# Padded staging rows for the weights, and an earlier order for tile 1's rows, means and two flags

## What is computed

```python
x = x + attention(layernorm(x), ctx, ctx, mask)     # causal mask and key mask, softmax over 256 keys
def ffn(x):                                          # x: (8, 256, 256), after a layernorm
    h = silu(tlin(x, w1, s1)) * tlin(x, w2, s2)      # 256 -> 1024
    h = gelu(tlin(h, h1, hs1))                       # 1024 -> 1024
    h = gelu(tlin(h, h2, hs2))                       # 1024 -> 1024
    return tlin(h, w3, s3)                           # 1024 -> 256
x = x + ffn(layernorm(x))                            # tlin(x, w, s) = (x @ w.T) * s
```

## Time and profile before

| | us |
|---|---|
| median of three timed executions | 370.94 (370.41 to 371.08) |
| the profiled execution's own time | 372.69 |
| its span, first to last instruction | 370.7 |
| TensorE matmul busy | 361.4 (98%) |
| TensorE weight load busy | 304.6 (82%) |
| VectorE busy | 177.9 (48%) |
| ScalarE busy | 147.0 (40%) |
| GpSimd busy | 33.9 (9%) |
| mean granted TensorE clock | 0.997 |

### The profile page before, as it was taken

How to read it: one execution, slowest core, us unless ns; L and a number is a source line. 1 busy time by engine, 2 the same in 40 slices (tenths; PEclk the granted TensorE clock), 3 DMA queues, 4 the chain that set the end, 5 groups by cost and what they waited for, 6 DMA issues and landing times.

```text
span 370.7 us, 4744 instructions
## 1 busy us (share of the span) xinstructions
PE 361.4 (98%) x1786; PEld 304.6 (82%) x1786; DVE 177.9 (48%) x405; ACT 147.0 (40%) x247; POOL 33.9 (9%) x59
## 2 busy tenths in 40 slices
PE   8899999999999999999999999999999999999994
PEld 7787887878798888888898888888889888888884
DVE  4857425245456652443655752434545652323323
ACT  4799743843135622251143642161122653121210
POOL 7450130000100031000000004000010000000000
PEclk9999999999999999999999999999999999999998
DMA  7899999992710001000331000000001000000001
GB/s 246 324 387 430 355 355 391 387 371 69 242 58 16 3 0 28 2 0 0 110 147 58 1 0 30 0 0 2 0 0 57 2 3 0 0 0 2 0 2 60
DMA packets 12739, 38.34 MB, mean 103 GB/s; under 512 B 2114, under 2 KB 5060, under 8 KB 12356
## 3 DMA queue, kind: packets, MB, share of 16 engines
q1 hardware_dynamic: 11840, 37.12, 27.2%
q10 hardware_dynamic: 868, 0.80, 0.8%
HBM read 35.80 MB, written 13.64 MB: 133 GB/s over the span
## 4 chain that ended last, share of the span: by engine, by line
PE 93%; DVE 3%; ACT 1%; issue 1%; POOL 0%; DVEq 0%; POOLq 0%
PE ring L975 60%; PE ring L949 15%; PE ring L994 8%; PE att L902 2%; PE att L921 2%; PE ring L1107 1%; PE att L892 1%; DVE turned L600 1%; PE att L910 1%; ACT work L476 0%; DVE x_attn L714 0%; DVE h_lo L657 0%; ACT act L517 0%; PE att L1134 0%; DVE h_hi L765 0%
## 5 line engine op out<-in xcount | busy, mean ns | idle before, releaser
L975 PE MATMUL ring<-h_hi,weights 128*128 128x512 f32 x512 | 201.5, 394 | 1.1 <-DVE seg_flags L739 0.9
L975 PE MATMUL ring<-h_lo,weights 128*128 128x512 f32 x512 | 199.4, 390 | 0.0
L975 PEld LDWEIGHTS ring<-h_hi,weights 128*128 128x128 f32 x512 | 96.1, 188 | 21.7 <-issue 1.6
L975 PEld LDWEIGHTS ring<-h_lo,weights 128*128 128x128 f32 x512 | 96.2, 188 | 19.7
L517 ACT ACTIVATE act<-ring,scales 128x512 f32<-128x512 f32 x64 | 44.1, 690 | 160.7 <-PE ring L975 157.2
L765 DVE CAST h_hi<-act 128x512 fp32r<-128x512 f32 x64 | 27.6, 430 | 145.8 <-ACT act L517 137.8
L657 DVE TENSOR_TENSOR h_lo<-act,h_hi 128x512 fp32r<-128x512 f32 x96 | 66.2, 689 | 2.6
L949 PE MATMUL ring<-xn_hi,weights 128*128 128x512 f32 (+1 forms) x140 | 51.6, 375 | 0.2 <-DVE xn_lo L733 0.2
L949 PE MATMUL ring<-xn_lo,weights 128*128 128x512 f32 (+1 forms) x140 | 51.1, 371 | 0.0
L505 ACT ACTIVATE gate<-ring,scales 128x512 f32<-128x512 f32 x32 | 22.0, 689 | 33.7 <-PE ring L949 33.6
L754 DVE SCALAR_TENSOR_TENSOR act<-ring,scales,gate 128x512 f32<-128x512 f32 x32 | 24.0, 749 | 17.4 <-PE ring L949 16.0
(11 more groups left out here) (128 smaller groups left out, 217.5 us busy)
## 6 DMA issues: line engine op xcount, KB each, us to landing
weights_staged<-in_weights SPq DMA_DIRECT2D x22, 512.0 KB, 8.7
weights<-weights_staged SPq DMA_DIRECT2D x22, 512.0 KB, 7.6
x_in<-in_x SPq DMA_DIRECT2D x8, 256.0 KB, 2.9
ctx_cols<-in_ctx_cols SPq DMA_DIRECT2D x8, 256.0 KB, 4.8
ctx_rows<-in_ctx_rows SPq DMA_DIRECT2D x4, 512.0 KB, 7.6
out_dram<-residual SPq DMA_DIRECT2D x16, 128.0 KB, 1.7
turned<-in_x_cols SPq DMA_DIRECT2D x3, 512.0 KB, 8.3
mask<-in_mask SPq DMA_DIRECT2D x3, 256.0 KB
```

What stands on the lines that cost most here:

```text
L975: ins = nc.tensor.matmul(bank[:], w, part[:, k].bitcast(dt), start=(k == 0 and part is h_hi[src]), stop=(k == HC - 1 and part is h_lo[src]))
```

## The change

The staging tensor gets rows of 1040 elements of which 1024 are used. Tile 1's rows are issued right behind raw piece 5, ahead of the load of piece 6. VectorE makes their statistics in the last four gate and up chunks of tile 0 (one row each), and their mean and variance after (0, 0). The means are stored at (0, 0) and spread at (0, 2); the queries are centred after (0, 5). The tests of pieces 14 to 21 each move one chunk forward (14 from (0, 6) to (0, 5), 15 and 16 from (0, 7) to (0, 6), 17 from (1, 0) to (0, 7), and so on). Flag HID2B is taken ahead of (1, 0) instead of (1, 1), and LAST ahead of (1, 6) instead of (1, 7). All of it concerns tile 0 alone, but for the row length.

```diff
-    staged_d = nc.dram_tensor("weights_staged", [PIECES, P, PIECE], F32).ap()
+    staged_d = nc.dram_tensor("weights_staged", [PIECES, P, PIECE + 16], F32).ap()[:, :, 0:PIECE]
 # SyncE
             load_raw(4)
             load_raw(5)
+            sp.wait_ge(x_attn_done, ROWS)
+            load_queries(1)
...
-                if n == FLAG_PIECES[HID1A][1]:
-                    sp.wait_ge(x_attn_done, ROWS)
-                    load_queries(1)
 # ScalarE
-                        if more and (layer, c) == (0, 2):
+                        if more and (layer, c) == (0, 0 if t == 0 else 2):
                             store_means(t + 1)
-                        if more and (layer, c) == (0, 3):
+                        if more and (layer, c) == (0, 2 if t == 0 else 3):
                             spread_means(t + 1)
...
-            after = ((0, 0), (0, 0), (0, 1), (0, 1), (0, 2), (0, 3), (0, 4), (0, 6), (0, 7), (0, 7), (1, 0), (1, 1),
-                     (1, 2), (1, 3), (1, 4))
+            after = ((0, 0), (0, 0), (0, 1), (0, 1), (0, 2), (0, 3), (0, 4), (0, 5), (0, 6), (0, 6), (0, 7), (1, 0),
+                     (1, 1), (1, 2), (1, 3))
 # VectorE
+            def next_stats(t, r):
+                if r % 2 == 0:
+                    dve.wait_ge(x_loaded[r // 2], 16 * (t + 1))
+                norm_stats(r, x_in)
...
+                    if t == 0 and c >= HC - ROWS and c < HC:
+                        next_stats(1, c - HC + ROWS)
...
-                        for flag, before in ((HID1B, (0, 2)), (HID1C, (0, 4)), (HID2A, (0, 7)), (HID2B, (1, 1)),
-                                             (HID2C, (1, 4)), (LAST, (1, 7))):
+                        for flag, before in ((HID1B, (0, 2)), (HID1C, (0, 4)), (HID2A, (0, 7)), (HID2B, (1, 0)),
+                                             (HID2C, (1, 4)), (LAST, (1, 6))):
...
-                        if at == (0, 1):
+                        if at == (0, 0 if t == 0 else 1):
                             wait_stats(t + 1, 0, ROWS - 1)
...
-                        if at == (0, 0):
+                        if t > 0 and at == (0, 0):
                             for r in range(ROWS):
-                                if r % 2 == 0:
-                                    dve.wait_ge(x_loaded[r // 2], 16 * (t + 2))
-                                norm_stats(r, x_in)
-                        if at in ((0, 1), (1, HID2_CHUNKS[2][0])):
+                                next_stats(t + 1, r)
+                        if at in ((0, 0 if t == 0 else 1), (1, HID2_CHUNKS[2][0])):
                             for r in range(ROWS):
                                 norm_moments(r)
-                        if at == (0, 6):
+                        if at == (0, 5 if t == 0 else 6):
                             for b in range(PAIR):
                                 centre(t + 1, b)
```

## The result

| | before | after |
|---|---|---|
| median of thirteen timed executions, us | 371.08 (369.82 to 372.92) | 368.97 (368.08 to 370.19) |
| profiled execution: own time, span, us | 372.69, 370.7 | 368.78, 366.6 |

The ratio after to before is 0.9937, with a 95% interval of 0.9917 to 0.9956: 2.3 us less, 1.6 to 3.1.

A forecast was written before the change was run, and what follows sets the result against it. TensorE was taken as the bound throughout (matmuls fill 361.4 of 370.7 us). Lost time -1.76, statistics +0.15 and raw piece 3 +0.06 sum to -1.55: from 370.94 to 369.4 us, range 368.8 to 370.7.

The forecast's parts named there:

- The lost time: TensorE's waits for late flags in tile 0 go: scores(1) 0.38, HID2B 1.03, LAST 0.35 us, together -1.76 us.
- The statistics: Four 0.35 us operations on VectorE in gate and up delay TensorE's matmul at 37.45: +0.15 us (0 to 0.6).
- Raw piece 3: Its load stands behind piece 7's slower staging and ScalarE waits for it: +0.06 us (0 to 0.7).
- The padding: Staging in 128 packets of 4 KB instead of 16 of 32 KB takes 0.12 us longer a piece (0 to 1.47).
- The means and tile 1's rows: Means stored and spread earlier, tile 1's rows issued 1.90 us ahead of piece 6's load with 4.0 us cover: cost 0.
- The cover of the tests: ScalarE's test of piece 17 may begin as late as 66.8, piece 17 landed at 60.8: 6.0 us of cover, cost 0.
- Rival C: Slow staging delays ScalarE's test of piece 17; kernel slower from 0.54 us more a piece, up to 384 us; chance 0.09.

The follow-up runs named there:

- e3: Kernel before with only the tests of pieces 14 to 21 and flags HID2B and LAST a chunk earlier: ratio 0.9950, compared trace stretch 1.75 us shorter.
- e4: Kernel before with only tile 1's rows, statistics, means and centring earlier: ratio 0.9986, compared trace stretch 0.47 us shorter.
- e7: Changed kernel with each of the four statistics in gate and up made twice: compared trace stretch 84.96 us, against 84.43 for the changed kernel.
- e5: Changed kernel with staging rows cut into runs of 256 elements, so packets of 1 KB: ratio to the kernel before 0.9943.
- e8: Changed kernel with chunks (0, 0) to (0, 2) in one branch instead of two: ratio to the kernel before 0.9944, compared trace stretch 2.39 us shorter.

## Why the prediction came out as it did

The mechanism was right: three late flags, two because VectorE took them behind work that waited for ScalarE, one because the centring stood in front; e3 and e4 part them as forecast, and nothing took the waits' place at these three. The size was low, 1.55 for 2.0, and the step that failed is the sum: each of its three terms was mis-sized, the first of them most.

- **The lost time, 1.76: measured 2.01.** I counted the distance between the last matmul and the next less 0.23. The distances did close as forecast (0.39, 1.03, 0.35). But the successor of a matmul behind a stop comes later too. In the kernel before, behind HID2B, the weight load and the two matmuls:

```profile
76.09 0.19 PEld L975 LDWEIGHTS ring<-h_hi,weights 128*128 128x128 f32 x1 [1.29 <-issue]
76.10 0.49 PE L975 MATMUL ring<-h_hi,weights 128*128 128x512 f32 x1 [0.88 <-DVE seg_flags L739]
76.43 0.40 PE L975 MATMUL ring<-h_lo,weights 128*128 128x512 f32 x1
```

  That is 0.33 behind 76.10, where 0.23 is usual. The weight load, else one distance ahead of its matmul, starts with it here. Matmul by matmul against the changed kernel, the successors give 0.11, 0.10 and 0.05 us beside the distances: 0.49, 1.15 and 0.38 at the three places, together 2.01. The page's idle times (0.22, 0.88, 0.20) are too low still, since the modelled ends cover part of the gap.
- **The statistics, +0.15: measured 0, at the place named by its slack and in the sum by luck.** What TensorE asks for, and when, was right: e7's weight load waits for the last low part. The end of that low part was wrong: 0.85 us later than before was forecast, and counted from the start of the stretch it is 0.43 later (12.34 for 11.91), because chunk 5's product began 0.36 earlier (6.84 for 7.20). That the edit didn't do; raw piece 4 was late in the execution profiled before and not in the one after (see e3). And the price has a place that the prediction didn't look at: the second statistic holds the flag HID1A back, 0.20 us on TensorE against e3. The late raw piece 4 had held the same flag as long in the kernel before, so the two cancel in the difference. Against an execution of the kernel before with raw piece 4 in time the change would gain some 1.75 us; that is an estimate from e3, of which there is one trace.
- **Raw piece 3, +0.06: measured 0.** The row of ScalarE's wait (1.14 us) was right, and it does sit at the edge of TensorE's path. But what moves it is the landing of that load, 0.2 to 2.1 us of wait from one execution to the next, padded or not.
- **The padding, 0.12 us a piece:** the four kernels without it average 100.9 us of engine time, the eight with rows of 1040 or 1088 and packets of 4 KB 102.1. That is 0.06 a piece, half the forecast, and the two groups overlap (100.3 to 101.7, 100.4 to 103.6). As it was covered, the sum didn't suffer.
- **The means and tile 1's rows:** right. The load of piece 6 is issued 1.1 us later (19.02), of its cover of 4.0; the centring is done at 61.2 as forecast. The cover of the tests was smaller than worked out, 3.1 us at piece 17 for 6.0, since piece 17 landed 1.5 us later than before and was tested at 65.37 and not at 66.8. Rival C's point was wrong by the other factor: not every microsecond of engine time reaches the landing (3.2 of 8.0 in e5).
- **The range:** its lower end allowed 0.35 us beyond 1.76 for the true gain but nothing for the scatter of the measurement, 0.7 us to either side. The 2.0 us of the stretch would give 368.9, just inside.

## What to carry to other kernels

Where one engine is the bound, look for places where the distance between starts of two of its instructions exceeds the usual one, and count the slower restart behind each as well. A flag that one engine computes and another branches on should be taken as soon as it can be, not where its taker's queue happens to be free: here 0.8 to 1.1 us pass between the written flag and the first dependent matmul, and they are free only if the flag is ahead by that much. Look at every flag behind the place where work is put, not only at the one that the work was meant for: the statistics cost nothing at the last low part and 0.2 us at HID1A. To tell half a microsecond in 370, compare a stretch of the trace between two fixed instructions; the span carries the chance of the first and the last transfers. A late load just ahead of the stretch can still reach into it, as raw piece 4 does here.

## What was not expected of the hardware

- The wait for the last store takes two sizes, 1.4 to 1.5 us (seven profiles beside the one before) or 3.1 to 3.7 (six, and the one before), for the same four transfers.
- DRAM to DRAM, a packet of 4 KB is nearly as cheap by byte as one of 32 KB (0.06 us a piece of 512 KB apart, on average over twelve kernels). Packets of 1 KB for staging and loading together cost 0.49 to 0.57 us a piece more, of 512 B 1.21 to 1.29.
- A read and branch whose flag is long known cost nothing at (0, 3) and some 0.4 us at (0, 2), right behind a sum; merging the branches took it away (e8). The sum alone isn't the reason: at (0, 4), (0, 7) and (1, 1) a sum stands ahead of the branch as well, and the matmul follows it after 0.14 us (49.54 to 49.68, 60.69 to 60.83, 70.84 to 70.98 after), against 0.55 at (0, 2). In the program only (0, 2) has a second wait ahead of the read, for the copied raw pieces (`pe.wait_ge(first_copied, RAW)` in `hid1`), long met. E8 takes out this wait together with the branch, so which of the two costs the 0.4 us stays open.
